# Disentangled attention and a routed feed-forward on one core: how the row maxima are turned, where loads are issued, and how the third norm reaches the logits

## The reference

```python
scores = jnp.einsum('bhqd,bhkd->bhqk', q, k) / scale
c2p = jnp.take_along_axis(c2p_att, c2p_pos, axis=-1)
p2c = swapaxes(jnp.take_along_axis(p2c_att, p2c_pos, axis=-1), -1, -2)
scores = scores + (c2p + p2c) / scale
probs = jax.nn.softmax(scores, axis=-1)
out = ctx @ Wo + bo + hidden_states
out = (out - mu) * jax.lax.rsqrt(var + 1e-7) * ln_scale + ln_bias
```

```python
x = x + _layernorm(_L0_attn_ref(_layernorm(x, axis=-1), ...), axis=-1)
x = x + _layernorm(_L0_ffn_ref(_layernorm(x, axis=-1), ...), axis=-1)
```

```python
routing_logits = (x @ Wr + br) / TEMPERATURE
indices = jnp.argmax(routing_probs, axis=-1)
h = jax.nn.relu(xi @ W1[i] + b1[i])
out = out + (h @ W2[i] + b2[i])
```

## Time and profile before

| | |
|---|---|
| time, median of 3 runs | 1785.49 us (1784.4 to 1792.77) |
| profiled execution | 1794.4 us, of which the span is 1792.3 |
| PE busy | 1615.2 us (90%), 13688 matmuls |
| DVE busy | 1364.4 us (76%) |
| ACT busy | 1145.8 us (64%) |
| POOL busy | 1030.9 us (58%) |
| granted clock of PE, mean | 0.946 |
| DMA moved | 421.65 MB, mean 235 GB/s |

### The profile page before, as it was taken

One profiled execution on the slowest core, in us unless ns is written; L12 is line 12 of the kernel. 1 busy time (PEld: TensorE's weight loads), 2 busy tenths in 40 slices (PEclk: granted clock), 3 DMA queues, 4 the chain that ended last, 5 costly groups with the idle time before them and its releaser, 6 DMA issues. The chain is left out here.

```text
span 1792.3 us, 41887 instructions
## 1 busy us (share of the span) xinstructions
PE 1615.2 (90%) x13688; PEld 1147.8 (64%) x13688; DVE 1364.4 (76%) x3868; ACT 1145.8 (64%) x2764; POOL 1030.9 (58%) x1264
## 2 busy tenths in 40 slices
PE   7963799999999999999999999999977866999997
PEld 4531566666666666666666666666634646999996
DVE  4753798999998999898899998999956754555553
ACT  6852587877877888878777878787754631222221
POOL 0003776777776777777777777777814622333332
PEclk9985899999999999999999999999997857999998
DMA  4986788878888788788888887888608616666762
GB/s 136 332 284 221 246 278 275 273 264 267 269 280 275 261 275 279 256 272 286 269 265 267 268 274 260 273 264 281 211 25 220 190 65 197 194 193 198 206 202 57
DMA packets 292450, 421.65 MB, mean 235 GB/s; under 512 B 35382, under 2 KB 233804, under 8 KB 292139
## 3 DMA queue, kind: packets, MB, share of 16 engines
q1 hardware_dynamic: 271640, 378.99, 65.2%
q10 hardware_dynamic: 16851, 30.67, 5.6%
q0 software_dynamic: 3744, 9.31, 1.4%
HBM read 241.39 MB, written 177.79 MB: 234 GB/s over the span
## 5 line engine op out<-in xcount | busy, mean ns | idle before, releaser
L934 ACT ACTIVATE t_probsT<-t_flip 128x512 f32<-128x512 f32 x1024 | 603.2, 615 | 192.3 <-PE t_flip L791 103.3
L851 DVE TENSOR_REDUCE t_most<-t_scores 128x1 f32<-128x640 f32 (+1 forms) x512 | 435.7, 851 | 120.1 <-PE t_scores L775 119.4
L997 POOL TENSOR_TENSOR t_near<-t_near,masks 128x384 f32<-128x384 f32 (+1 forms) x128 | 146.5, 1144 | 275.5 <-DMA t_near<-skew_d 274.8
L861 DVE CUSTOM_DVE_ANT_0 t_band<-t_scores,t_near,t_most 128x384 f32<-128x384 f32 (+1 forms) x512 | 297.0, 580 | 0.5 <-DVE t_most L851 0.2
L872 DVE TENSOR_SCALAR_CACHE_REDUCE t_band<-t_band,t_top 128x384 f32<-128x384 f32 (+1 forms) x512 | 291.2, 569 | 0.0
L926 ACT COPY t_table<-t_table_ps 128x388 f32<-128x388 f32 x502 | 251.2, 500 | 54.1 <-PE t_table_ps L747 50.9
L812 PE MATMUL t_sum_ps<-t_probsT,vals 128*32 128x256 f32 x4096 | 274.3, 385 | 0.3 <-ACT t_probsT L934 0.3
L1013 POOL TENSOR_TENSOR t_near<-t_near,masks 128x768 f32<-128x768 f32 (+1 forms) x128 | 268.6, 2098 | 0.0
L775 PE MATMUL t_scores<-masks,t_near 128*128 128x128 f32 x1408 | 244.8, 278 | 19.6 <-POOLq L1016 18.8
L798 PE MATMUL t_flip<-masks,t_band 128*128 128x128 f32 x1408 | 258.1, 274 | 0.0
L768 PE MATMUL t_scores<-afters,quests 105*128 105x256 bf16 (+3 forms) x1024 | 244.3, 288 | 3.8 <-DVE t_top L861 3.6
(11 more groups left out here) (212 smaller groups left out, 2572.4 us busy)
## 6 DMA issues: line engine op xcount, KB each, us to landing
skew_d<-t_table SPq DMA_DIRECT2D x128, 1024.0 KB, 11.3
t_near<-skew_d SPq DMA_DIRECT2D x128, 640.0 KB, 8.0
t_near<-skew_d SPq DMA_DIRECT2D x128, 384.0 KB, 7.4
e_w<-in_L_ffn_W_dram ACTq DMA_DIRECT2D x39, 512.0 KB
e_w<-in_L_ffn_W_dram SPq DMA_DIRECT2D x39, 512.0 KB
split_d<-p_part SPq DMA_DIRECT2D x32, 384.0 KB, 3.3
afters<-split_d SPq DMA_DIRECT2D x128, 96.0 KB
quests<-split_d SPq DMA_DIRECT2D x128, 96.0 KB
```

The lines of the kernel that those rows point to most:

```text
L851: nc.vector.tensor_reduce(most[:, c:c + 1], out[:, wide:S], AX.X, ALU.max).then_inc(far_seen, 1)
L861: nc.vector.tensor_tensor_reduce(band[n % 2][:, t, 0:wide], out[:, 0:wide], near[n % 2][:, 0, t, at:at + wide], 1.0, most[:, c:c + 1], ALU ...
L934: nc.scalar.activation(probsT[s % 4][:, half * 512:(half + 1) * 512], flip_ps[half][:, :], ACT.Exp, scale=SCALE).then_inc(expd, 1)
```

## The change

It has these parts:

- **Maxima.** The turn leaves PE and ACT. DVE's `turn_top(n)` makes four `nc.vector.transpose` of 32 x 32 bf16 blocks behind `look(8n+9)`. For that `top_part` gets a fourth part, set to 0 by POOL once, and `topT` has 32 rows. ACT's `send_top(n)` only issues the transfer, at step 8n+10 rather than 8n+9. The bf16 identity and PE's wait on `top_kept` go.
- **Loads.** `EARLY` is 3: unit 2 is loaded in `project` at step 6, and `load_far(0)` moves to step 7. `wo` is loaded in `attend` at unit 12 and has its own semaphore.
- **b1** comes in as 64 contiguous rows and is turned by PE at step 2 of `mix`, beside a matmul that sums `wr` over its rows.
- **Third norm.** It is no longer applied to x. PE turns `x2` itself, one step earlier, and the logits are `row_inv * (x2 @ wr) + row_shift * wr_sum + br`, with one root, reciprocal and shift for all rows at the end. ACT and DVE run 18 of the 20 steps' norms, and `xf` is gone.
- **Aggregates.** `mv`, which the shift of the norms reads (L1251), is in PSUM.

```diff
-EARLY = 2
+EARLY = 3
...
+                    hats.load_unit(sp, split_d, 2)
+                if s == 7:
...
-        top_part = [sb(f"top_part{i}", [P, PARTS, QT], BF16) for i in range(2)]
-        topT = [sb(f"topT{i}", [PARTS * QT, P], BF16) for i in range(2)]
+        top_part = [sb(f"top_part{i}", [P, 4, QT], BF16) for i in range(2)]
+        topT = [sb(f"topT{i}", [4 * QT, P], BF16) for i in range(2)]
...
-                if EARLY <= u + 2 < N and u % FARS == 0:
+                if FARS <= u + 2 < N and u % FARS == 0:
...
+                if u == 12:
+                    sp.dma_start(wo[:, :, :], Wo.rearrange("(k p) n -> p k n", p=P)).then_inc(wo_in, 16)
...
-                if x >= AHEAD and (x - AHEAD) % QT == 2:
-                    pe.wait_ge(top_kept, (x - AHEAD) // QT)
...
-            def turn_top(n):
-                pe.wait_ge(split_made, 5 * (n + 1))
-                pe.wait_ge(table_kept, by_act(min(n * QT + QT + AHEAD + 2, TS) - 1))
-                nc.tensor.matmul(table_ps[0:PARTS * QT, 0, 0:P],
-                                 top_part[n % 2][:, :, :].rearrange("p a t -> p (a t)"), ident16[:, :],
-                                 start=True, stop=True).then_inc(top_turned, 1)
-
...
-                if s > QT and s % QT == 1 and s // QT <= N:
-                    turn_top(s // QT - 1)
...
-            nc.vector.tensor_copy(ident16[:, :], masks[:, 4, :]).then_inc(ident_made, 1)
+            def turn_top(n):
+                dve.wait_ge(split_made, 5 * (n + 1))
+                if n < 2:
+                    dve.wait_ge(parts_set, 2)
+                if n >= 2:
+                    dve.wait_ge(top_in[(n - 2) % BUFS], 16 * ((n - 2) // BUFS + 1))
+                for a in range(4):
+                    last = nc.vector.transpose(topT[n % 2][:, 32 * a:32 * a + 32],
+                                               top_part[n % 2][32 * a:32 * a + 32, :, :].rearrange("p a t -> p (a t)"))
+                last.then_inc(top_turned, 1)
+
...
+                if s > QT and s % QT == 1:
+                    turn_top(s // QT - 1)
+            turn_top(N - 1)
...
-            def keep_top(n):
+            def send_top(n):
-                if n >= 2:
-                    act.wait_ge(top_in[(n - 2) % BUFS], 16 * ((n - 2) // BUFS + 1))
-                nc.scalar.copy(topT[n % 2][:, :], table_ps[0:PARTS * QT, 0, 0:P]).then_inc(top_kept, 1)
-                act.wait_ge(top_kept, n + 1)
-                nc.scalar.dma_start(quest[n % BUFS][MROW:ROWS, :], topT[n % 2][:, :]).then_inc(top_in[n % BUFS], 16)
+                nc.scalar.dma_start(quest[n % BUFS][MROW:ROWS, :], topT[n % 2][0:PARTS * QT, :]).then_inc(top_in[n % BUFS], 16)
...
-                if s > QT and s % QT == 1 and s // QT <= N:
-                    keep_top(s // QT - 1)
+                if s > QT and s % QT == 2 and s // QT <= N:
+                    send_top(s // QT - 1)
...
+            for i in range(2):
+                nc.gpsimd.memset(top_part[i][:, PARTS:4, :], 0.0).then_inc(parts_set, 1)
...
-        y1, y4, y5, x2, xf = ([sb(f"{w}_{i}", [P, G, D]) for i in range(BUFS)] for w in ("y1", "y4", "y5", "x2", "xf"))
+        y1, y4, y5, x2 = ([sb(f"{w}_{i}", [P, G, D]) for i in range(BUFS)] for w in ("y1", "y4", "y5", "x2"))
-        stats, mv = sb("stats", [P, 2, 3, G, 6]), sb("mv", [P, 2, 3, G, 2])
-        root, inv, shift = (sb(w, [P, 2, 3, G]) for w in ("root", "inv", "shift"))
+        stats, mv = sb("stats", [P, 2, 3, G, 6]), ps("mv", [P, 2, 2, G, 2])
+        root, inv, shift = (sb(w, [P, 2, 2, G]) for w in ("root", "inv", "shift"))
+        row_mv = sb("row_mv", [P, NT, 2])
+        row_root, row_inv, row_shift = (sb(w, [P, NT]) for w in ("row_root", "row_inv", "row_shift"))
+        wr_sum, offset = sb("wr_sum", [P, E]), sb("offset", [P, NT, E])
+        b1_rows, aside_ps = sb("b1_rows", [E * KC, P]), ps("aside_ps", [P, E * KC + E])
...
-            loads = [(wo[:, :, :], Wo.rearrange("(k p) n -> p k n", p=P)),
-                     (ls_b[:, :], row(ln_s, D)), (lb_b[:, :], row(ln_b, D)),
+            loads = [(ls_b[:, :], row(ln_s, D)), (lb_b[:, :], row(ln_b, D)),
-            assert len(loads) == 6
+            assert len(loads) == 5
-            for dst, src in [(b1_sb[:, :, :], b1.rearrange("e (c p) -> p e c", p=P)), (b2_sb[:, :], b2),
+            for dst, src in [(b1_rows[:, :], b1.rearrange("e (c p) -> (e c) p", p=P)), (b2_sb[:, :], b2),
-                    sp.wait_ge(const_in, 48)
+                    sp.wait_ge(aside_kept, 1)
...
+                if s == E - 2:
+                    dve.wait_ge(aside_made, 1)
+                    nc.vector.tensor_copy(wr_sum[:, :], aside_ps[:, E * KC:E * KC + E])
+                    nc.vector.tensor_copy(b1_sb[:, :, :].rearrange("p e c -> p (e c)"), aside_ps[:, 0:E * KC]
+                                          ).then_inc(aside_kept, 1)
-                    dve.wait_ge(const_in, 48)
+                    dve.wait_ge(aside_kept, 1)
...
-                for i in range(lo, hi):
+                if hi > 2:
+                    g = s - 2 * LAG
+                    for t in range(G):
+                        last = nc.vector.bn_aggr(row_mv[:, g * G + t, :], stats[:, c, 2, t, :])
+                    last.then_inc(row_mv_made, 1)
+                if s >= NORMED:
+                    continue
+                for i in range(lo, min(hi, 2)):
+                hi = min(hi, 2)
...
-            dve.wait_ge(loaded, 16 * 6)
+            dve.wait_ge(loaded, 16 * 5)
+            dve.wait_ge(row_root_made, 1)
+            nc.vector.reciprocal(row_inv[:, :], row_root[:, :]).then_inc(row_norm, 1)
+            dve.wait_ge(row_norm, 1)
+            nc.vector.scalar_tensor_tensor(row_shift[:, :], row_mv[:, :, 0], -1.0, row_inv[:, :], ALU.mult, ALU.mult
+                                           ).then_inc(row_norm, 1)
+            dve.wait_ge(row_norm, 2)
+            nc.vector.tensor_tensor(offset[:, :, :], wr_sum[:, :].unsqueeze(1).to_broadcast([P, NT, E]),
+                                    row_shift[:, :].unsqueeze(2).to_broadcast([P, NT, E]), ALU.mult).then_inc(row_norm, 1)
+            dve.wait_ge(row_norm, 3)
+            nc.vector.tensor_tensor(offset[:, :, :], offset[:, :, :], br_b[:, :].unsqueeze(1).to_broadcast([P, NT, E]), ALU.add
+                                    ).then_inc(row_norm, 1)
+            dve.wait_ge(row_norm, 4)
-                                         br_b[:, :].unsqueeze(1).to_broadcast([P, NT, E]), ALU.add))
+                                         row_inv[:, :].unsqueeze(2).to_broadcast([P, NT, E]), ALU.mult))
+            link(nc.vector.tensor_tensor(logits[:, :, :], logits[:, :, :], offset[:, :, :], ALU.add))
-            assert count[0] == 5
+            assert count[0] == 6
...
-                    a = max(lo, 1)
-                    last = nc.scalar.activation(root[:, c, a:hi, :], mv[:, c, a:hi, :, 1], ACT.Sqrt, bias=eps[:, 1:2])
+                    last = nc.scalar.activation(root[:, c, 1, :], mv[:, c, 1, :, 1], ACT.Sqrt, bias=eps[:, 1:2])
-                if s >= 2 * LAG + 1:
-                    keep_xf(s - 2 * LAG - 1)
+                if s >= TURN:
+                    keep_xf(s - TURN)
-                for i in range(lo, hi):
+                for i in range(lo, min(hi, 2)):
-                    src, dst = ((y1, y4), (y4, y5), (x2, xf))[i]
+                    src, dst = ((y1, y4), (y4, y5))[i]
-                    if i == 2 and g >= BUFS:
-                        act.wait_ge(xf_turned, g - BUFS + 1)
-            keep_xf(NG - 1)
+            for g in range(NORMED - TURN, NG):
+                keep_xf(g)
+            act.wait_ge(row_mv_made, NG)
+            nc.scalar.activation(row_root[:, :], row_mv[:, :, 1], ACT.Sqrt, bias=eps[:, 1:2]).then_inc(row_root_made, 1)
...
-                pe.wait_ge(norm_made[2], g + 1)
+                pe.wait_ge(x2_made, g + 1)
-                                                   xf[g % BUFS][:, t, k * P:(k + 1) * P], ident)
+                                                   x2[g % BUFS][:, t, k * P:(k + 1) * P], ident)
...
-            pe.wait_ge(loaded, 16 * 6)
+            pe.wait_ge(wo_in, 16)
-            for s in range(STEPS + 2):
+            for s in range(NG + TURN + 1):
-                g = s - 2 * LAG - 1
+                if s == 2:
+                    pe.wait_ge(loaded, 16 * 5)
+                    pe.wait_ge(const_in, 48)
+                    nc.tensor.transpose(aside_ps[:, 0:E * KC], b1_rows[:, :], ident[0:E * KC, 0:E * KC])
+                    for k in range(2):
+                        last = nc.tensor.matmul(aside_ps[:, E * KC:E * KC + E], masks[:, 3, :], wr[:, k, :],
+                                                start=(k == 0), stop=(k == 1))
+                    last.then_inc(aside_made, 1)
+                g = s - TURN
-            pe.wait_ge(sorting, 6)
+            pe.wait_ge(sorting, 7)
...
-                        pool.wait_ge(norm_made[2], g - BUFS + 1)
+                        pool.wait_ge(xf_turned, g - BUFS + 1)
```

(32 more changed lines are left out.)

## The result

The changed kernel takes 1827.05 us (median of 4 runs, 1821.48 to 1829.82) against 1787.93 us for the kernel before. The ratio is 1.0213, 95% interval 1.0176 to 1.025. So the change makes the kernel slower by some 2%, where 1753 us and faster was forecast, and the time lies above the forecast's range of 1740 to 1770 and above the wider one that ends at 1810.

The account below looks back on a forecast made before the run. PE was taken to bound attend and the chain through the norms mix; -12 +5 -3.5 -4.2 -2.2 -8.5 -7.0 = -32.4 took 1785.5 to 1753 us, range 1740 to 1770 (wider range 1732 to 1810).

Parts of the forecast that it names:

- When the maxima are sent: In attend: 4.0 us left from ACT's issue to the flip, transfer takes 4 us or less in most units; +5 us.
- The first rival: In attend: the sent maxima come too late, PE stalls 2.3 us in each of 64 units, 1907 us; chance 0.17.
- Its middle case: The first rival with a transfer of 4.9 us, so 0.9 us of stall in each of 64 units: 1818 us.
- PE's relief, -12: In attend: turning the maxima on DVE frees PE of 24 us, half lost to DVE's extra 29 us; -12 us.
- Transposes waiting for POOL: Rival in attend: DVE's transposes wait for POOL's operation until 719.1, leaving 3.0 us; 1810 us, chance 0.06.
- Loads moved, -3.5: Head of attend: unit 2's loads leave SP's queue there, so the skew write starts some 3 us earlier; -3.5 us.
- Head of mix, -4.2: Start of mix: PE's first matmul waits for bo_part rather than the last of six loads; -4.2 us.
- The rest of mix, -2.2, -8.5 and -7.0: Mix: shorter b1 transfer, -2.2 us; warm steps from 4.94 to about 4.2 us, -8.5; earlier logits, -7.0.
- the third rival: Mix keeps its time: granted clock stays low, gains halve, 1761 us; chance 0.11 for mix or attend giving less.
- The aggregates in PSUM: In mix: the norms' shift falls from 1.18 to some 0.2 us without POOL's hold, part of the steps' -8.5 us.

Follow-up runs that it names:

- e6: The change with DVE turning the maxima ahead of look(8n+9) and ACT sending them behind the first exponential of step 8n+10; 1760.59 us, ratio 0.9812.
- e7: e6 with the flips 14 steps behind the scores instead of 13; 1765.0 us, ratio 0.988.
- e1: The change with only the maxima turned as before (PE matmul, ACT copy and transfer at step 8n+9); 1768.96 us, ratio 0.9888.
- e4: The change with the flips 14 steps behind the scores instead of 13; 1789.19 us, ratio 0.9996.
- e5: The kernel before with only the maxima turned by DVE and sent a step later; 1847.64 us, ratio 1.0336.
- e10: e1 with the aggregates (mv) in SBUF again instead of PSUM; 1763.56 us, ratio 0.9866.
- e3: The change with only ACT's sending of the maxima one step earlier, DVE's turn still behind look(8n+9); 1959.04 us, ratio 1.0947.
- e2: The change with DVE turning the maxima ahead of look(8n+9) and ACT sending them at step 8n+9; 1775.63 us, ratio 0.9898.
- e11: e6 with six heads buffers in mix instead of four; 1751.82 us, ratio 0.9813.

## Why the prediction was wrong, point by point

**The failed step is "When the maxima are sent".** The term "4 us or less in most units", +5 us in all, was mis-sized. The place and the point of decision were well chosen, but what stood on either side of the point was off. The window was 3.6 us and not 4.0, as the four transposes take 0.83 us and not 0.45. And the transfer took 5.1 us until PE went on (median 5.2), not 4 or less. That was in the trace of before: there no transfer of the 56 units had its last packet sooner than 4.5 us behind the issue, and the median was 5.5. Because PE asked only after 6.5 us, no wait showed it, except in the late cases of the earlier trace rows, which the forecast took for an upper bound and which were nearly the usual case.

The gap in the traffic was no reason for 4 us. In that same unit q10 was silent through the gap and moved its packets from 719.6 on. In the change a gap helped where it came earlier: 11 of the 56 units have a DMA share under 0.4 from 1 to 3 us behind the issue, and there the packets start after 1.9 to 3.1 us. (In `e6` 7 units have such a gap, and they start after 3.1 to 4.1, so the gap alone doesn't settle it.) One of the 11 was issued at 814.74, and its flip waited for nothing. These are its packets from 817.00 to 817.60, and a window ahead of them:

```profile
q10 hardware_dynamic: 27, 0.01, 4.8%
```
```profile
815.74:817.74 2.00, 1.97 (x26) 1.11 (x19) 2.00 (x6) 2.00 (x6) 2.00 (x3) 1.00 0.19 62
```

What fills the 4 us in the other units stays open. The Trainium skill, "DMA: Bandwidth & Descriptors", "Latency and other measured facts", on which the forecast drew, has a fixed cost of about 2 us and an HBM latency that grows at high load. The 2 us don't agree with the 4.0 us ahead of the first packet here, and the measurement decides. HBM's latency by itself no run here shows.

The first rival, given 0.17, is what happened, at about 1.6 us a stalled unit (87.0/54) and not 2.3. Its middle case, 1818, was 9 us off. That closeness is partly luck. It took 0.9 us of stall a unit, and a unit did grow by 0.86; but the stalls of PE are 87 us and the units grew by 54, and what took back the other 33 isn't shown. And mix gave 9.5 us less than its terms.

**PE's relief, -12.** Not there by the units. With the transfer nearly in time (`e6`, `e7`) units take 17.67 and 17.78 us, with PE's turn 17.68. In both some wait of ACT or PE for the maxima is left, and the ratio of `e6` is 0.8% under that of `e1`, so how much of the 24 us a perfect placing would give stays open. The transposes cost 53 us of DVE (64 x 0.83), nearer the upper bound than the 29 assumed, and DVE is 96 us of 100 busy at the end of `attend` in `e6`. That DVE paid for PE's saving fits these rows, but no run takes DVE's part away, so it is likely and not shown.

**Transposes waiting for POOL.** They never did: 193 to 204 ns over 256 of them. This rival fell.

**Loads moved, -3.5.** Right, and a little more: 5.3 us, by the first issue of the maxima at the same step (195.55 to 190.25 in `e1`).

**Head of mix, -4.2.** Right: PE starts 5.4 us behind the block's first issue (1393.31-1387.93) instead of 9.4 (1349.22-1339.78), -4.1.

**The rest of mix, -2.2, -8.5 and -7.0.** The mechanisms were right. A warm step falls to 3.6 (1418.15 to 1421.74) to 4.4 us, and the last x2 to logits from 9.6 to 4.6. The sum was too high in the profiled run: -8.3 of -17.7. The missing part lies with the clock, the third rival as a part. The same mix code took 104.4, 93.5, 106.5, 96.2, 104.1, 99.5 and 95.1 us in seven profiles (the change, `e1` to `e4`, `e6`, `e7`). Two of them, `e1` first:

```profile
1326.60:1420.10 93.50, 79.80 (x421) 57.46 (x421) 66.19 (x285) 49.63 (x114) 59.65 (x48) 0.79 0.76 230
```
```profile
1334.60:1441.10 106.50, 91.76 (x421) 65.53 (x421) 66.40 (x285) 49.59 (x114) 59.55 (x48) 0.71 0.66 202
```

The same 421 matmul rows take PE 79.8 us at a mean clock of 0.79 and 91.8 at 0.71, while DVE's work is alike. So old and new are compared at like clocks. At 0.70 and 0.71 they take 116.8 and 104.4 us (before, the change), and at 0.79 they take 113.2 and 93.5 (`e5`, `e1`). With the head's 4.2 the forecast had -21.9, and these are -12.4 and -19.7. At the higher clock it was nearly right. At the lower one PE's own work seems to take part of the gain; this is one pair of profiles each.

**The aggregates in PSUM** were one of the causes named for a shorter step. The rows of the shift came out as said: 159 to 163 ns with `mv` in PSUM, 160 to 1235 ns in SBUF. The trace agrees with the Trainium skill, "SBUF — State Buffer", "SBUF: two separate sides", by which a VectorE operation with two SBUF inputs and one of GpSimd exclude each other. But alone (`e1` against `e10`) they gave no time that shows; with the heads ahead some 6 us appear, in one profile each.

## What to carry to other kernels

That a transfer makes nobody wait doesn't say that it is quick: a small transfer that a later step needs is costed by its own packets in the old trace (here 4.0 us to the first, 5.5 to the last), and not from a quiet moment of the DMA engines. Moving work off the busiest engine can be worth nothing if the engine that alternates with it takes the work; compare the two idle shares first. And place the producer before choosing where the transfer is issued: the turn 1.67 us earlier, with the sending at a point where its engine has just finished an operation of the same step, turned +2.1% into -1.9%.

## What the runs showed that was not expected

- A 32 x 32 bf16 transpose on DVE takes 199 ns for a thousand elements, and a 128 x 256 f32 one 440 ns. Cutting one up costs nearly by count.
- A wait of ACT of up to 3.9 us in one place of most units (184.1 us in 51 places) made units of 20.84 us out of the change's 18.67 (`e3`), although ACT is the third busiest engine.
- The 6 KB of the maxima had their first packet 4.0 us behind the issue by the median in nine kernels (4.00 to 4.10: before, the change, `e1`, `e2`, `e4` to `e7`, `e11`). In the kernel before that held for all 56 units (3.8 to 4.2), although a gap in the traffic opened 2 us behind the issue.
- Identical code of a block took 93.5 to 106.5 us in profiles of kernels that differ only in the block before it, with the granted clock at 0.71 to 0.79 on the mean. An edit in mix worth less than 10 us can't be read from one profile.
- After PE's second wait for heads the granted clock was 0.50 from 1429.2 to 1453.0 us, and PE was busy 23.80 of these 23.80 us. A wait of 1.75 us thus came before some three steps of 7.1 us each.
